# A scan-and-convolution kernel: the transposes of the history moved into the recurrence, fewer filler products, and the convolution's TensorE program written as a loop

## The reference

```python
# 1. a tanh recurrence over 512 steps, one state of 256 channels per sequence
xw = einsum('ntd,dh->nth', x, Wx) + b
h_t = tanh(xw_t + h_(t-1) @ Wh)                      # u = all h_t
# 2. a causal convolution of each channel along time, kernel K made from 64 decays
K[c, t] = sum_n C_re[c, n] * exp(-exp(A_log[n]) * exp(log_dt[c]) * t)
x = x + (u convolved with K) + u * D
# 3. a gated normalised recurrence (cumulative sums), then a shared MLP and 16 experts, top 2
x = x + ffn(gates(x, cond))
```

## Time and profile before

| | us |
|---|---|
| median of 3 runs | 989.84 |
| the profiled execution | 987.75 |
| its span | 985.9 |
| recurrence, to the first transpose of u | 0 to 379.6 |
| transposes of u | 379.6 to 388.3 |
| convolution | 388.3 to 462.3 |
| gates, shared MLP, experts | 462.3 to 985.9 |

### The profile page before, as it was taken

The page is one execution under the profiler, slowest core; times in us unless marked ns, Lnnn a source line. Parts: engine busy times, 40 slices in busy tenths (PEclk is TensorE's granted clock), DMA queues, the critical chain, the costliest instruction groups (busy, mean ns, idle before and its releaser), DMA issues.

```text
span 985.9 us, 64681 instructions
## 1 busy us (share of the span) xinstructions
PE 919.4 (93%) x28784; PEld 774.4 (79%) x28784; DVE 411.2 (42%) x781; ACT 518.1 (53%) x1819; POOL 283.1 (29%) x310
## 2 busy tenths in 40 slices
PE   7999999999999998777999999999999999999993
PEld 5888888888888887666444445788899999999993
DVE  1000011000110004432698899875564655646450
ACT  2444444444444446662776776333465656656551
POOL 3111111111111111220001543762035455463545
PEclk6799999999999999998999999999999999999997
DMA  2222223221111110001000211343266666575634
GB/s 87 86 86 90 95 86 106 95 67 40 38 35 32 32 38 23 5 5 49 0 1 12 75 36 37 98 187 121 70 179 149 124 158 136 132 159 130 130 39 54
DMA packets 67163, 76.96 MB, mean 78 GB/s; under 512 B 24001, under 2 KB 53334, under 8 KB 67106
## 3 DMA queue, kind: packets, MB, share of 16 engines
q1 hardware_dynamic: 52226, 58.51, 19.1%
q0 software_dynamic: 14592, 17.10, 10.5%
q10 hardware_dynamic: 288, 0.56, 0.2%
HBM read 44.16 MB, written 33.83 MB: 79 GB/s over the span
## 4 chain that ended last, share of the span: by engine, by line
PE 85%; issue 5%; DVE 4%; ACT 4%; POOL 1%; DMA 0%; POOLq 0%; ACTq 0%; DVEq 0%
PE ps L503 19%; PE ps L789 17%; PE ps L495 8%; PE ps L803 8%; PE ps L655 8%; PE ps L705 6%; PE ps L476 6%; PE ps L732 3%; ACT tok L857 2%; PE ps L592 2%; PE ps L714 2%; PE ps L583 2%; PE ps L568 2%; PE ps L481 2%; POOL out L453 1%
## 5 line engine op out<-in xcount | busy, mean ns | idle before, releaser
L503 PE MATMUL ps<-tok,wh 128*32 128x8 f32 x16384 | 255.7, 180 | 12.9 <-issue 3.7
L857 ACT ACTIVATE tok<-ps 128x8 f32<-128x8 f32 x1024 | 156.3, 178 | 203.8 <-PE ps L503 199.5
L503 PEld LDWEIGHTS ps<-tok,wh 128*32 128x32 f32 x16384 | 220.4, 112 | 48.2 <-ACT tok L857 25.0
L453 POOL DMA_INDIRECT out<-arena,dest x80 | 127.9, 1599 | 99.2 <-ACT arena L1002 76.9
L476 PE MATMUL ps<-zero 128*32 128x192 bf16 x1920 | 141.4, 255 | 0.0
L789 PE MATMUL ps<-xgT_hi,ew_hi 128*128 128x320 f32 (+1 forms) x384 | 119.4, 311 | 2.9 <-DVE spare L1247 1.6
L407 POOL TENSOR_TENSOR big<-tok,zero 128x128 f32 x64 | 29.1, 455 | 322.0 <-ACT tok L857 322.0
L789 PE MATMUL ps<-xgT_hi,ew_lo 128*128 128x320 f32 (+1 forms) x384 | 119.6, 311 | 0.0
L789 PE MATMUL ps<-xgT_lo,ew_hi 128*128 128x320 f32 (+1 forms) x384 | 118.9, 310 | 0.0
L1115 DVE TENSOR_TENSOR arena<-arena,pack 128x256 f32 x32 | 13.6, 426 | 246.4 <-ACT arena L862 246.4
L1353 DVE TENSOR_TENSOR mid<-mid,ps 128x320 f32<-128x320 f32 (+1 forms) x96 | 46.7, 487 | 106.5 <-ACT mid L1020 64.4
(11 more groups left out here) (203 smaller groups left out, 1647.2 us busy)
## 6 DMA issues: line engine op xcount, KB each, us to landing
slots_in<-mid SPq DMA_DIRECT2D x16, 645.0 KB, 3.7
mid<-slots_in SPq DMA_DIRECT2D x16, 645.0 KB, 4.2
arena<-in_ex_down SPq DMA_DIRECT2D x16, 384.0 KB
arena<-in_ex_gate SPq DMA_DIRECT2D x16, 352.0 KB
arena<-in_ex_up SPq DMA_DIRECT2D x16, 352.0 KB
xst<-in_x_steps SPq DMA_DIRECT2D x66, 64.0 KB, 1.8
xtok<-in_x_tok SPq DMA_DIRECT2D x16, 256.0 KB, 2.7
mid<-k_pad SPq DMA_DIRECT2D x32, 128.0 KB, 3.1
```

What stands on the lines that cost most here:

```text
L453: pool.indirect_dma_start(out=out[:, :], out_offset=bass.IndirectOffsetOnAxis(ap=dest[:, z, t:t + 1], axis=0), in_=yo[:, z, t], in_offset= ...
L503: last = nc.tensor.matmul(sums_at(bank, t, o)[Q * j:Q * j + Q], wh[:, k, columns(j, o)], hring[:, (n - 1) % (2 * G), k], start=False, stop ...
L857: nc.scalar.activation(hring[:, n, o], sums_at(n // G, n % G, o), ACT.Tanh).then_inc(s_h[o], 1)
```

## The change

Four edits, in two parts.

1. *Recurrence.* The history `uT` gets another layout, so that the 128 x 128 piece of one sequence and one block of 64 steps is contiguous, and block tb stands at place (tb+1) mod 8. In each pass VectorE copies two pieces of the block before to `pair`, TensorE turns them at step 4 (`two_turned`, into bank 6), and VectorE copies the result out to `u_tok`; after the last pass only the last block's eight transposes are left. The ring `hring` moves from `tok` to `arena`, since `u_tok` is now written during the recurrence, and the identity is loaded at the start.
2. *Fewer products of zeros.* `keep_groups_up(192)` stays in 5 steps of a pass (0, 2, 10, 12, 14) instead of 15. The kernel's sums are split over steps 7 and 8.
3. *Convolution.* TensorE's program is a loop of 8 iterations of two rounds. The rounds of a parity read the same places: `tz`, `u_tok` and `qd` of groups 0 and 1. Group m >= 2 is brought there: `tz` by a DMA of SyncE (14 of 256 KB), `u_tok` and `qd` by copies of ScalarE (28 of 128 x 512). The order within a round is own_block(m), block_states(m+1), carried(m); a small product (`stand`) carries the waits ahead of each part. One block_states more runs at the end, whose result nobody reads.
4. The scan's decays `d0` are made by GpSimd in 14 instructions of 128 x 512 instead of by ScalarE in 112 of 128 x 64.

```diff
-        uT = big[:, :].rearrange("p (n k t b) -> p n k t b", n=NB, k=C, b=B)
+        uT = big[:, :].rearrange("p (n b k t) -> p n b k t", n=NB, k=C, b=B)
+        uTp = big[:, :].rearrange("p (v t) -> p v t", t=P)
-        hring = tok[:, 7168:7168 + 2 * G * C * B].rearrange(...)
+        hring = part(9216, [2 * G, C, B])
+        pair = part(9728, [2, P])
...
@@ SyncE, after the Toeplitz blocks are in
+            for m in range(2, NCH):
+                sp.wait_ge(s_own, m - 1)
+                sp.dma_start(tz[:, CP * (m % 2):CP * (m % 2) + CP], tz[:, CP * m:CP * m + CP]).then_inc(s_slot_tz[m % 2], 16)
...
@@ GpSimd, convolution
                 pool.wait_ge(s_tmm, m - 1)
                 power_args(m)
+                pool.wait_ge(s_xc, m)
+                block_decays(m)
...
@@ TensorE, a step of the recurrence
+            def two_turned(i):
+                pe.wait_ge(s_pair, i + 1)
+                for j in range(2):
+                    last = nc.tensor.transpose(ps[:, 6, P * j:P * j + P], pair[:, j], ident[:])
+                last.then_inc(s_utr, 1)
-                    if n != G - 1:
+                    if n in (0, 2, 10, 12, 14):
+                        if n == 10:
+                            pe.wait_ge(s_uev, i + 1)
                         keep_groups_up(192)
+                    if n == 4:
+                        two_turned(i)
                     if n == G - 1:
-                        kernel_sums()
+                        kernel_sums(0)
+                    if n == G:
+                        kernel_sums(1)
...
@@ TensorE, after the recurrence
-            for n in range(2 * NB):      # 64 transposes through 4 banks
+            for bq in range(2):          # 8 transposes into 2 banks
...
@@ TensorE, convolution
-            for m in range(NCH):
-                if m + 1 < NCH:
-                    block_states(m + 1)
-                own_block(m)
-                carried(m)
+            with pe.Fori(0, NCH // 2) as i:
+                for z in range(2):
+                    m = 2 * i + z
+                    pe.wait_ge(s_x1, m + 1)
+                    pe.wait_ge(s_slot_tz[z], 16 * i + 16)
+                    stand()
+                    own_block(z)
+                    pe.wait_ge(s_pe, m + 2)
+                    pe.wait_ge(s_xc, m + 1)
+                    pe.wait_ge(s_uea, 2 * m + SLOTS - 1)
+                    stand()
+                    block_states(1 - z)
+                    pe.wait_ge(s_xc, m + 2)
+                    pe.wait_ge(s_uea, 2 * m + SLOTS - 2)
+                    stand()
+                    carried(z)
...
@@ ScalarE, convolution
             for m in range(2, NCH):
-                block_decays(m)
                 powers(m)
+                steps_to_slot(m)         # waits for own_block(m - 2)
+                decays_to_slot(m)        # waits for carried(m - 2)
...
@@ VectorE, a pass of the recurrence
+                    dve.wait_ge(s_hist, 2 * i + 2)
+                    nc.vector.tensor_copy(pair, uTp[:, bass.ds(2 * i, 2)]).then_inc(s_pair, 1)
                     kernel_states(i)
                     decays_out(i)
+                    dve.wait_ge(s_utr, i + 1)
+                    u_out(copied, 6, bass.ds(...), max(tb, 1) - 1).then_inc(s_uev, 1)
                     kernel_out(i)
```

More of the change, by code:

```diff
@@ L268, in columns, with slot_of, u_out @@
             return slice(P * o + Q * j, P * o + Q * j + Q)
-        def u_out(engine, copy, half, done):
-            for n in range(half, 2 * NB, 2):
-                tb, bq = n // 2, n % 2
-                engine.wait_ge(s_utr, n + 1)
-                copy(u_tok.rearrange("p c (b t) -> p c b t", t=NB)[:, :, 4 * bq:4 * bq + 4, tb],
-                     ps[:, 2 + n % 4, :].rearrange("p (b c) -> p c b", b=4)).then_inc(done, 1)
+        def slot_of(tb):
+            return (tb + 1) % NB
+        def u_out(copy, bank, b0, columns_of_b):
+            n = 4 if bank != 6 else 2
+            return copy(u_tok.rearrange("p c (b t) -> p c b t", t=NB)[:, :, b0, columns_of_b], ps[:, bank, 0:n * P].rearrange("p (b c) -> p c b", b=n))
         @block.sync
@@ L406, in keep @@
                 pool.wait_ge(s_h[1], 2 * G * i + G * half + G + 1)
-                pool.tensor_tensor(uT[:, tb, :, bass.ds(i * (-2 * G) + (HB * (tb + 1) - G - G * half), G), :], group, zeros, ALU.add).then_inc(s_hist, 1)
+                pool.tensor_tensor(uT[:, slot_of(tb)].rearrange("p b k t -> p k t b")[:, :, bass.ds(i * (-2 * G) + (HB * (tb + 1) - G - G * half), G), :], group, zeros, ALU.add).then_inc(s_hist, 1)
             for tb in range(NB):
```

114 lines of the change are left out of this document (66 added, 48 removed).

## The result

The changed kernel takes 1101.85 us (median of 4 runs, 1100.6 to 1103.07) where before took 989.07 (4 runs beside it, 986.16 to 991.02): ratio 1.1143, 95% interval 1.1111 to 1.1175. It is 11% slower, where 953 us and "faster" were forecast, and lies outside the range. The profiled execution has a span of 1098.7 us, 112.8 more than before.

A forecast was written before the change was run, and what follows sets the result against it. The circle products, tanh, products bounds the recurrence, PSUM copies the turning, arriving program the convolution. From 987.75 us, -24.2 - 6.4 - 5.3 - 1.0 = -36.9 gives 950.9; the median 2.1 above it, 953 us, range 938 to 980.

The forecast's parts named there:

- the clock falls in the recurrence: Rival: with ten of fifteen groups of zeros gone from each pass, the clock falls, +79 us, 1030 us; chance 0.09.
- convolution as a loop: Convolution: looped rounds, with waits, branches and first fetching, take 49.7 us where 73.9 stood, -24; bounds 46 to 58.
- turning, first transpose to first product: Between recurrence and convolution: only eight transposes, a copy and a handover remain, about 2.4 us; -6.4 us in all.
- a pass: Recurrence: a pass falls from 11.28 to 11.1 us, net -0.17 each, -5.3 over 31 passes; bounds -9 and +3.
- two transposes at step 4, net: Recurrence, step 4: two transposes replace nothing but hide partly behind inputs, costing between 0 and 0.22 us, taken as 0.11.
- packets of the instruction queue there: Between the end of the recurrence and the gates: the instruction queue brings 3 to 5 packets, not 19.
- first pass: First pass of the recurrence, at the pace of arriving program: 38 matmuls and their loads fewer save 1 us.
- The reading of the stops as arriving program: Convolution before: 16 TensorE stops, 19.1 us, come from instruction packets arriving every 3.9 us.
- refetching rival: Rival, convolution: the loop is fetched again at each of seven returns, 27 us, 981 us in all; chance 0.12.
- Another engine sets the round: Rival, convolution: ScalarE's copies or an uncovered chain make a round 3.3 us instead of 2.8, 961 us; chance 0.11.
- the wait itself: Convolution loop: three waits with `stand` a round cost at most 0.15 us each, 0 to 7 us, taken as 2.
- Split sums: Recurrence, steps 7 and 8: four sums become two and two, taking back 0.13 of the 0.15 us behind step 7.

The follow-up runs named there:

- Experiment 2: Bursts of 30 products of zeros (512 columns) after every eighth pass, added to the kernel before with zeros in 5 steps (1029.93 us) and to the changed kernel (1053.42 us).
- change with bursts: The changed kernel plus a burst of 30 products of zeros of 512 columns after every eighth pass: 1053.42 us in one run.
- kernel of few zeros: The kernel before with zeros only in steps 0, 2, 10, 12 and 14 of a pass, nothing else changed: 1077.74 us, ratio 1.0918.
- loop alone: The kernel before with only the convolution's loop added, three `stand` a round, recurrence and turning as before: 973.75 us, ratio 0.9888.
- recurrence part alone: The kernel before with early transposes (to bank 4) and split sums, all zeros kept and the convolution written out: 989.46 us, ratio 1.0004.

## Why the prediction was wrong

**The step that failed** is the weighing of the rival "the clock falls in the recurrence", given 0.09. Its argument was that the convolution kept 0.91 of the clock with TensorE busy 53 of 74 us, and that the recurrence without ten groups of zeros is "far denser, since inputs, sums or zeros still follow the products in 15 of the 16 steps". Two faults. First, the rows compared a clock that was being *held* with one that had to be *raised*: both kernels start slow (634 ns a product of 512 columns from 1.7 us on), before's clock is 0.50 from 8.2 to 35.5 us, and the only row on rising was the 8 us without a gap at 27.5 to 35.5, with zeros in 15 of 16 steps. Experiment 2 shows the two questions have different answers. Second, busy time was taken for density: 32 records of state products, 176 ns each in the median, stand in 0.50 us of before's timeline, so busy records overlap. The prediction itself had said in its first paragraph that busy is no proof.

**The rival's mechanism was right, its price low.** It put 0.86 us on a step at clock 0.50 and 13.8 on a pass, +79 us. Its 0.16 us for 192 columns agrees with the 0.427 for 512 above. Plain steps take 0.81 to 0.83, but a pass takes 14.33, mostly since the step behind the transposes takes 1.44 there: 3.2 over the forecast pass, 100 us where 79 stood. And it left the convolution out, which ran at 0.50 as well (a round 5.97 us, and parts of 1.98 to 2.01 as in the change with bursts, where 0.50 is in the list): 23.4 longer than before, where 24.2 shorter was forecast, 48 us by the forecast's terms. 1030 + 21 + 48 is 1099, and the profiled execution took 1100.6.

**The transposes** play no part in the sign: fewer zeros alone cost 91 us, and the recurrence's part with all zeros, transposes and turning together, cost nothing (ratio 1.0004). At 0.50 they do cost more than at 1.00: the step behind them takes 1.44 us, where the kernel of few zeros without them takes 0.81; at 1.00 it is 1.01 against 0.67. In the kernel of few zeros the clock rose 5.0 us into a stretch of transposes alone (465.4 to 470.4), so there they didn't keep it down.

Term by term, with the clock at 1.00 but for the two rows from the kernel after:

| term | forecast | measured | from |
|---|---|---|---|
| convolution as a loop | 49.7, bounds 46 to 58 | 59.4 | loop alone |
| turning, first transpose to first product | 2.4 | 2.27 | change with bursts |
| a pass | 11.1 | 11.10, later up to 11.28 | change with bursts |
| two transposes at step 4, net | 0.11, bound 0.22 | 0.34 among all zeros, 0.27 in the change with bursts | recurrence part alone; change with bursts |
| packets of the instruction queue there | 3 to 5 | 3 | after |
| first pass | -1 | -0.1 | after |

*Convolution.* The reading of the stops as arriving program is borne out: 19 packets became 3, and the stops are gone. The refetching rival (0.12) falls with them: three packets serve seven returns. "Another engine sets the round" fell too: no wait in the loop names one. What was mis-sized is the wait itself: 2 us for 48 of them, with 0.15 each as the upper bound from the loop's end in the recurrence. They cost 0.27 each on average, 13 us in all (48 times), and taking one out of a round saved 0.25. With seven branches at 0.2, 44.2 + 13.1 + 1.4 = 58.7 of the 59.4. The branch's 0.15 was no bound for a stop between dense products, where the `stand` started 1.06 us behind the part ahead of it, 0.08 before that part's end, and the next part 0.11 behind the `stand`.

*Passes.* 11.10 agrees because errors cancel. Split sums alone make 11.02 of 11.28, 0.26 where 0.13 was forecast: neither step of 0.82 is left in a pass. That behind step 15 went too, which the split doesn't explain (in the recurrence part alone, also split, it is 0.83 at 201 us and 0.76 in most later passes); why is open. Six groups of zeros less are another 0.23 (11.02 to 10.79) where 0.15 was forecast. The transposes cost 0.27 in this kernel where 0.11 was. So -0.26 - 0.23 + 0.27 = -0.22, where -0.13 - 0.15 + 0.11 = -0.17 was forecast and -0.18 measured. Three terms were each off by 0.08 to 0.16, and that their sum came out is luck.

*First pass.* It ran at the low clock in both kernels (before 0.50 from 8.2 us on, after 201 ns a state product) and ends at 28.03 us instead of 28.14. A microsecond can't be read here: two kernels with the same recurrence, before and the loop alone, end it at 28.14 and 27.00.

*Open.* Why three stops a round keep the convolution at 0.50 and two don't, and why three don't either behind 64 transposes: the runs show which kernels fall, not by what rule. Of two kernels one execution in four held, which no row of their traces explains.

## What to carry to other kernels

Filler products (products of zeros) had two jobs here, raising the clock (at 35.5 us with 15 groups a pass, not by 471.3 with five) and holding it (88 us with five); ask of each group that you take out which job it did, and read the answer from a stretch where the clock rises, not from one where it stays. A clock row ahead of the trace's first entry said 1.00 here where the products were those of 0.50 (201 ns a state product up to 471.3 us, first entry at 579.7): take the duration of one unchanged matmul before and after (176 and 201 ns here), and compare the mean clocks of several executions (0.993 and 0.732 here, at the same time). A wait placed between dense small matmuls cost 0.24 to 0.34 us each time here, so put several conditions into one stop, and expect a whole-array instruction that is moved among column strips to cost more than its own length (0.34 us a pass here, where 0.22 was the forecast's bound).

## What the runs showed of the hardware

- Written out, TensorE's 2560 small products of the convolution took 74 us, with 19 packets of program and 16 stops on no other engine (19.1 us). As a loop of two rounds (some 650 instructions) they brought 3 packets in 100 us, and no such stop within the loop. The gain is 14.5 us of 74, although each round got three stops; up to 6.8 of it can be the clock, which was 0.91 there and 1.00 in the loop.
- The same recurrence stayed at 0.50 for 119 us (460 us without bursts), and at 1.00 for 88 us at a time behind 6.4 us of dense products. The clock rose 5.0 us into transposes alone where it had not risen in that recurrence.
- At 0.50 a state product's record grows only from 176 to 201 ns, while a part of the convolution takes 1.98 us instead of 1.17. The convolution's back-to-back products took 1.7 times as long, the recurrence's plain step, which waits for ScalarE in between, a fifth more (0.67 to 0.81 us).
- One `stand` of 8 columns less a round, 0.25 us each, moved a kernel by 41 us, through the clock (1053 us in one run, 1012 in four; the convolution at 0.50 in the one profiled and at 1.00 in the other).
